# Three tiles of a row selection in f32r parts made on GpSimd, marks written on two engines, and a look-up one step earlier

## The reference

```python
gates = softmax(xf @ w_router + b_router)
topv, topi = top_k(gates, 2)                      # two experts per token
pos = cumsum(onehot)[...] - 1                     # running slot in each expert
keep = pos < cap                                  # cap = int(1.25 * 1184 / 8) = 185
buf = zeros(e, cap, d).at[e_flat, posc].add(where(keep, xf[tok], 0))
h = gelu(einsum('ecd,edf->ecf', buf, w1) + b1)    # 256 -> 1024
out = einsum('ecf,efd->ecd', h, w2) + b2          # 1024 -> 256
y = zeros.at[tok].add(w * out[e_flat, posc])      # weighted sum of the two experts
```

## Time and profile before

| | before |
|---|---|
| median of 3 runs, us | 159.71 (159.04 to 161.41) |
| span of the profiled execution, us | 157.9 |
| PE busy, us (share) | 148.0 (94%) |
| DVE busy | 105.5 (67%) |
| ACT busy | 82.8 (52%) |
| POOL busy | 50.9 (32%) |
| mean granted clock of PE | 0.989 |

### The profile page before, as it was taken

One profiled execution on the slowest core, in us unless ns is written; L12 is line 12 of the kernel. 1 busy time (PEld: TensorE's weight loads), 2 busy tenths in 40 slices (PEclk: granted clock), 3 DMA queues, 4 the chain that ended last, 5 costly groups with the idle time before them and its releaser, 6 DMA issues.

```text
span 157.9 us, 2961 instructions
## 1 busy us (share of the span) xinstructions
PE 148.0 (94%) x982; PEld 138.4 (88%) x982; DVE 105.5 (67%) x330; ACT 82.8 (52%) x210; POOL 50.9 (32%) x55
## 2 busy tenths in 40 slices
PE   7999999999999979999999999999999999999950
PEld 6548999899789768899799899999999999999940
DVE  0074994769887898981396859669486694785710
ACT  3222754644317998857066557474682665737100
POOL 6001200505530000005437167084371661604361
PEclk9999999999999999999999999999999999999995
DMA  5999960079000345301499897888868978600422
GB/s 169 406 420 435 394 230 0 0 243 338 5 0 22 138 163 184 116 0 28 97 349 292 272 269 194 269 192 307 269 130 270 262 250 264 131 7 0 48 25 23
DMA packets 16978, 28.46 MB, mean 180 GB/s; under 512 B 1133, under 2 KB 13591, under 8 KB 16585
## 3 DMA queue, kind: packets, MB, share of 16 engines
q1 hardware_dynamic: 14505, 25.49, 46.6%
q0 software_dynamic: 2464, 2.86, 10.6%
HBM read 24.21 MB, written 4.14 MB: 180 GB/s over the span
## 4 chain that ended last, share of the span: by engine, by line
PE 65%; DMA 11%; DVE 7%; ACT 6%; issue 3%; POOL 3%; SPq 1%; POOLq 1%; DVEq 0%
PE ps L1298 20%; PE ps L1333 10%; PE ps L1132 6%; PE ps L1223 6%; DMA w_even<-w 5%; DMA first_t<-first 4%; PE ps L1335 4%; PE ps L1240 3%; ACT xn L556 2%; PE ps L1165 2%; PE ps L1343 2%; PE ps L1310 2%; DMA rows_in<-xrows,src_row 2%; PE ps L1261 2%; ACT xn L565 2%
## 5 line engine op out<-in xcount | busy, mean ns | idle before, releaser
L497 POOL DMA_INDIRECT out_rows<-out_s,dst_row x16 | 23.8, 1485 | 38.4 <-ACT out_s L682 32.1
L658 ACT ACTIVATE first_t<-ps,b_cur 128x186 f32<-128x186 f32 x64 | 23.0, 413 | 23.5 <-PE ps L1298 22.0
L1333 PE MATMUL ps<-hid_hl,split 128*128 128x372 f32 x96 | 29.1, 369 | 0.0
L1335 PE MATMUL ps<-hid_hl,split 128*128 128x186 f32 x96 | 23.9, 249 | 0.0
L1298 PE MATMUL ps<-first_t,patch_t 128*128 128x186 f32 x128 | 21.7, 322 | 0.1
L977 DVE CAST hid_hl<-first_t 128x372 fp32r<-128x372 f32 x28 | 10.7, 383 | 15.9 <-ACT first_t L658 15.9
L1298 PEld LDWEIGHTS ps<-first_t,patch_t 128*128 128x128 f32 x128 | 20.1, 190 | 0.4 <-issue 0.4
L482 POOL DMA_INDIRECT rows_in<-xrows,src_row x14 | 15.6, 1113 | 11.0 <-DVE src_row L945 7.1
L1298 PE MATMUL ps<-first_t,w_even 128*128 128x186 f32 x112 | 18.9, 321 | 0.0
L522 ACT ACTIVATE split<-patch_t 128x512 fp32r<-128x512 f32 (+2 forms) x28 | 14.4, 577 | 8.1 <-DMA patch_t<-patches 5.7
L1335 PEld LDWEIGHTS ps<-hid_hl,split 128*128 128x128 f32 x96 | 18.3, 191 | 0.0
(11 more groups left out here) (179 smaller groups left out, 263.2 us busy)
## 6 DMA issues: line engine op xcount, KB each, us to landing
w_even<-w SPq DMA_DIRECT2D x8, 1024.0 KB, 5.7
patch_t<-w SPq DMA_DIRECT2D x8, 1024.0 KB, 5.5
att<-attn SPq DMA_DIRECT2D x1, 1280.0 KB, 9.4
patch_t<-patches SPq DMA_DIRECT2D x1, 1188.0 KB, 14.0
patch_t<-patches SPq DMA_DIRECT2D x1, 1080.0 KB, 11.5
first_t<-first SPq DMA_DIRECT2D x1, 978.0 KB, 7.0
out_rows<-h SPq DMA_DIRECT2D x2, 384.0 KB, 2.5
xrows<-xn SPq DMA_DIRECT2D x2, 384.0 KB, 3.5
```

The costliest lines, as they stand in the source:

```text
L497: pool.indirect_dma_start(out=out[:, :], out_offset=bass.IndirectOffsetOnAxis(ap=dst_row[0:SIZES[s], c:c + 1], axis=0), in_=out_s[q][0:SIZ ...
L658: ins = act.activation(hid[:, f, :], bank(pair)[:, (f % 2) * SL:(f % 2 + 1) * SL], ACT.Gelu, bias=b1_cur[q][:, f:f + 1])
L1333: pe.matmul(dst[:, 0:2 * SL], w2_h[q][:, f, cols], hid_hl[:, f].rearrange("p a s -> p (a s)"), start=f == 0, stop=False)
L1335: ins = pe.matmul(dst[:, 0:SL], w2_l[q][:, f, cols], hid_hl[:, f, 0], start=False, stop=f == KF - 1)
```

## The change

Tiles 6, 7 and 8 are selected in f32r: POOL copies each of them to a high part and subtracts that from the tile for a low part, as soon as ACT has written the tile; PE multiplies both parts by a one-hot matrix in f32r. The tiles of the second part come in the order 5, 9, 6, 7, 8, both halves of each together. In `ACT_ORDER`, `keep2` of E goes in front of `rows2` of C. POOL also writes `at_p` of tiles 7 and 8, the summand of L1028 and the first weight part; DVE writes `at_p` of the others and the last two weight parts, and its small operations on the weights move up by one place. ACT's load of the Gelu table goes behind its copy of half 1. The look-up goes in front of pair 3 of the first layer, and waits for POOL's writes too.

```diff
+PICK_PARTED = (6, 7, 8)
+PLACES = [*range(6), 9, *PICK_PARTED]
+BY_POOL = (7, 8)
...
+        pick_h, pick_l = (split[i][0:TT, 0:len(PICK_PARTED) * D].rearrange("p (t d) -> p t d", d=D) for i in (2, 3))
+        onehot_r = split[3][0:TT, len(PICK_PARTED) * D:len(PICK_PARTED) * (D + SL)].rearrange("p (t s) -> p t s", s=SL)
...
-                     ("rows2", B_), ("squares2", C), ("root2", C), ("rows2", C), ("keep2", E), ("rows2", E), ("keep2", C)]
+                     ("rows2", B_), ("squares2", C), ("root2", C), ("keep2", E), ("rows2", C), ("rows2", E), ("keep2", C)]
...
+            for i, t in enumerate(PICK_PARTED):
+                if t == GROUPS[C][0]:
+                    pool.wait_ge(row_made, 1)
+                elif t < GROUPS[E][0]:
+                    done(pool, ("rows2", C))
+                else:
+                    pool.wait_ge(row_made, 2)
+                pool.tensor_copy(pick_h[:, i], xn[:, t]).then_inc(row_high, 1)
+                pool.wait_ge(row_high, i + 1)
+                pool.tensor_tensor(pick_l[:, i], xn[:, t], pick_h[:, i], ALU.subtract).then_inc(row_split, 1)
+
+            pool.wait_ge(slots_fixed, 1)
+            for t in BY_POOL:
+                for k in range(2):
+                    pool.tensor_scalar(at_p[:, t, k], iota_slot[:, 0:ST], slot_p[:, t, k:k + 1], None, ALU.is_equal
+                                       ).then_inc(pool_marked, 1)
+            pool.wait_ge(places_known, 1)
+            for c in range(1, ID_SUM):
+                start = ids.rearrange("p (t c a b) -> p t c a b", c=ID_SUM, a=1, b=1)[:, :, c]
+                pool.tensor_tensor(marks[:, :, :, 1 + c], at_q, start.broadcast_to((TT, NT, 2, SC)), ALU.mult
+                                   ).then_inc(pool_marked, 1)
+            pool.wait_ge(first_part, 1)
+            pool.tensor_tensor(marks[:, :, :, ID_PARTS], at_q, spread(parts[:, :, :, 0], NT, SC), ALU.mult
+                               ).then_inc(pool_marked, 1)
...
-            act.activation(idle[:, :], eps_col[0:1], ACT.Gelu)
-
             act.wait_ge(picked, KD)
             copy(buf_t[0][:, 1:], pick_slot[:, 1:]).then_inc(half_ready, 1)
+
+            act.activation(idle[:, :], eps_col[0:1], ACT.Gelu)
...
-                for t in range(t0, t0 + n):
-                    dve.tensor_scalar(onehot[:, t], iota_slot[:, 1:SL + 1], place0[:, t:t + 1], None, ALU.is_equal
+                for t in PLACES[t0:t0 + n]:
+                    dst = onehot_r[:, PICK_PARTED.index(t)] if t in PICK_PARTED else onehot[:, t]
+                    dve.tensor_scalar(dst, iota_slot[:, 1:SL + 1], place0[:, t:t + 1], None, ALU.is_equal
...
             take_in(0, 0, first=True)
-            find_slots(0, 2)
+            find_slots(0, 1)
             behind(m)
             m = marked(dve.reciprocal(got[:, :], got[:, :]))
-            dve.wait_ge(places_known, 1)
-            for c in range(1, ID_SUM):
-                start = ids.rearrange("p (t c a b) -> p t c a b", c=ID_SUM, a=1, b=1)[:, :, c]
-                dve.tensor_tensor(marks[:, :, :, 1 + c], at_q, start.broadcast_to((TT, NT, 2, SC)), ALU.mult)
+            find_slots(1, 2)
+            behind(m)
+            m = marked(dve.tensor_tensor(weight[:, :, :], weight[:, :, :], per_token(got[:, :], 2), ALU.mult))
             find_slots(2, 3)
             behind(m)
-            m = marked(dve.tensor_tensor(weight[:, :, :], weight[:, :, :], per_token(got[:, :], 2), ALU.mult))
+            dve.tensor_copy(parts[:, :, :, 0], weight[:, :, :]).then_inc(first_part, 1)
             find_slots(3, 4)
...
-            find_slots(7, 9)
+            find_slots(6, BY_POOL[0])
             behind(m)
             m = part_of(2)
-            find_slots(9, NT)
+            find_slots(BY_POOL[-1] + 1, NT)
             behind(m)
-            for k in range(2):
-                ins = dve.tensor_tensor(marks[:, :, k, ID_PARTS:],
...
+            dve.wait_ge(places_known, 1)
+            for c in range(1, PARTS):
+                ins = dve.tensor_tensor(marks[:, :, :, ID_PARTS + c], at_q, spread(parts[:, :, :, c], NT, SC), ALU.mult)
             ins.then_inc(marks_ready, 1)
...
                 pe.wait_ge(pool_set, 10)
+                pe.wait_ge(pool_marked, 2 * len(BY_POOL) + ID_SUM)
...
-                pick_tiles(range(t0 - HELD, t0), range(KD))
-                for k in range(KD):
-                    pick_tiles(range(t0, t0 + c), [k]).then_inc(picked, 1)
+                pick_tiles([*range(t0 - HELD, t0), *(t for t in PLACES[t0:] if t not in PICK_PARTED)], range(KD))
+                for i, t in enumerate(PICK_PARTED):
+                    pe.wait_ge(onehot_ready, PLACES.index(t) + 1)
+                    pe.wait_ge(row_high, i + 1)
+                    for k in range(KD):
+                        pe.matmul(pick_slot[:, k, :], pick_h[:, i, k * 128:(k + 1) * 128], onehot_r[:, i, :],
+                                  start=False, stop=False)
+                    pe.wait_ge(row_split, i + 1)
+                    for k in range(KD):
+                        ins = pe.matmul(pick_slot[:, k, :], pick_l[:, i, k * 128:(k + 1) * 128], onehot_r[:, i, :],
+                                        start=False, stop=t == PICK_PARTED[-1])
+                        if t == PICK_PARTED[-1]:
+                            ins.then_inc(picked, 1)
...
                     up(e, q, pair, not first)
+                if first:
+                    look_up(bank(MARKS_BANK)[0:ST, 0:(ID_PARTS + PARTS) * SC])
                 up(e, q, PAIRS - 1, not first)
                 if first:
-                    look_up(bank(MARKS_BANK)[0:ST, 0:(ID_PARTS + PARTS) * SC])
```

More of the change, by code:

```diff
@@ L264, in vit_block @@
         onehot_ready, picked = sem("onehot_ready"), sem("picked")
+        row_made, row_high, row_split = sem("row_made"), sem("row_high"), sem("row_split")
         places_known, rows_marked = sem("places_known"), sem("rows_marked")
+        slots_fixed, first_part, pool_marked = sem("slots_fixed"), sem("first_part"), sem("pool_marked")
         marks_ready, marks_looked, src_ready, dst_ready = (
@@ L566, in normalise @@
                                          bias=nmr[0:r, base + t:base + t + 1], scale=rstd[0:r, base + t:base + t + 1])
+                    if base and t in PICK_PARTED and i < n - 1:
+                        ins.then_inc(row_made, 1)
                 return ins
@@ L1012, in _ @@
             behind(n)
-            n = marked(dve.tensor_tensor(slot_p[:, :, :], slot_p[:, :, :], lost[:, :, :], ALU.add))
+            dve.tensor_tensor(slot_p[:, :, :], slot_p[:, :, :], lost[:, :, :], ALU.add).then_inc(slots_fixed, 1)
             behind(m)
             m = marked(dve.tensor_tensor(got[:, :], weight[:, :, 0], weight[:, :, 1], ALU.add))
-            behind(n)
+            dve.wait_ge(slots_fixed, 1)
             dve.tensor_tensor(at_q[:, :, :, :], grid(iota_slot[:, 0:SC], NT, 2, SC), spread(slot_q[:, :, :], NT, SC), ALU.is_equal
@@ L1021, in _ @@
             take_in(0, 0, first=True)
-            find_slots(0, 2)
+            find_slots(0, 1)
             behind(m)
             m = marked(dve.reciprocal(got[:, :], got[:, :]))
-            dve.wait_ge(places_known, 1)
-            for c in range(1, ID_SUM):
-                start = ids.rearrange("p (t c a b) -> p t c a b", c=ID_SUM, a=1, b=1)[:, :, c]
-                dve.tensor_tensor(marks[:, :, :, 1 + c], at_q, start.broadcast_to((TT, NT, 2, SC)), ALU.mult)
+            find_slots(1, 2)
+            behind(m)
+            m = marked(dve.tensor_tensor(weight[:, :, :], weight[:, :, :], per_token(got[:, :], 2), ALU.mult))
             find_slots(2, 3)
             behind(m)
-            m = marked(dve.tensor_tensor(weight[:, :, :], weight[:, :, :], per_token(got[:, :], 2), ALU.mult))
+            dve.tensor_copy(parts[:, :, :, 0], weight[:, :, :]).then_inc(first_part, 1)
             find_slots(3, 4)
-            behind(m)
-            m = part_of(0)
+            dve.wait_ge(first_part, 1)
+            m = rest_after(0)
             find_slots(4, 5)
             behind(m)
-            m = rest_after(0)
+            m = part_of(1)
             find_slots(5, 6)
             behind(m)
-            m = part_of(1)
-            find_slots(6, 7)
-            behind(m)
             m = rest_after(1)
-            find_slots(7, 9)
+            find_slots(6, BY_POOL[0])
             behind(m)
             m = part_of(2)
-            find_slots(9, NT)
+            find_slots(BY_POOL[-1] + 1, NT)
             behind(m)
-            for k in range(2):
-                ins = dve.tensor_tensor(marks[:, :, k, ID_PARTS:],
-                                        at_q[:, :, k].rearrange("p t (a q) -> p t a q", a=1).broadcast_to((TT, NT, PARTS, SC)),
-                                        parts[:, :, k].rearrange("p t (c a) -> p t c a", a=1).broadcast_to((TT, NT, PARTS, SC)),
-                                        ALU.mult)
+            dve.wait_ge(places_known, 1)
+            for c in range(1, PARTS):
```

(17 more changed lines are left out.)

## The result

The changed kernel took 163.11 us (median of 4 runs, 160.94 to 164.35), the kernel before 159.38 beside it (4 runs). The ratio is 1.0146 [1.0096, 1.0197]: slower, by less than 2%. Two of the four executions (163.84, 164.35) had a granted clock of 0.97 in the mean, as some executions of the kernel before have too; the ratio leaves these out, the median doesn't. The profiled execution took 160.94, with a span of 159.1 against 157.9. On the page POOL's busy time rises from 50.9 to 58.2 us and PE's falls from 148.0 to 147.4.

A forecast was written before the change was run, and what follows sets the result against it. Bound by DVE's string up to the take-in, then by whether marks are ready for PE. Terms 1.5 + 0.3 + 1.6 - 0.3 = +3.1 us, span near 161.0, time 162.8; forecast's own range 161.6 to 164.2, overall range 159.6 to 164.9.

The forecast's parts named there:

- held in front, free behind: Rival: the parts cost 1.15 before the take-in, POOL's marks run freely behind it, look-up waits 0.3; 161.2 us, chance 0.20.
- A two-operand DVE operation stands until POOL's has ended.: Between 60 and 70 us, DVE operations with two SBUF operands stand still until the POOL operation in progress ends.
- The parts, +1.5.: Ahead of the take-in, POOL's three copies and three subtracts hold DVE's string: +1.5 us (1.15 to 1.85).
- Pick on PE, 0.: The f32r pick on PE, even if shorter, gains 0, since the take-in was not waiting for it.
- POOL's is_equal in front of the take-in, +0.3.: POOL's first is_equal holds the next small DVE operation in front of the take-in: +0.3 us (0 to 0.7).
- The wait at the look-up, 1.6: Marks come 5.8 after the take-in, PE is at the look-up 4.16 after it: PE waits 1.6 (0 to 3.0).
- 2.56 held: Behind the take-in, POOL's three is_equal (0.8) and two products (1.76) hold DVE for 2.56, about 0.3 of it harmless.
- What POOL's marks give.: DVE's marks work gets 1.33 shorter by durations, about 1.1 with overlap, but POOL's operations among it hold DVE.
- The look-up earlier, -0.3.: Ahead of pair 3: no wait for gathered rows, expert 2's weights load earlier, expert 1's output wait goes; -0.3 (-0.6 to 0).
- The clock, rival at 0.18.: Rival: PE idle before the first layer lowers its clock, up to +2.4; 164.5 us, 165.2 at the outside, chance 0.18.

The follow-up runs named there:

- e1: The change without POOL's copies and subtracts, tiles picked in f32 as before; POOL's marks and the earlier look-up stay: 159.64 us, ratio 1.0027.
- e10: e1 with POOL's three copies and three subtracts put back, their results read by nobody: 160.77 us, ratio 1.0104.
- e2: The change with DVE writing the marks that POOL writes there; POOL's copies and subtracts and the earlier look-up stay: 161.80 us, ratio 1.0105.
- e8: e5 with two more filler products on PE ahead of the first part of the pick: 159.57 us, ratio 1.0001.
- e9: The change with two more filler products on PE ahead of the first part of the pick: 161.55 us, ratio 1.0081.
- e6: The kernel before, with the look-up in front of pair 3 and nothing else: 160.58 us, ratio 1.0006.
- e5: The change without POOL's copies and subtracts, POOL keeping only the four is_equal of at_p; DVE writes the marks products: 159.57 us, ratio 0.998.
- e7: The kernel before, with four unread is_equal of 128x96 added on POOL near 32 us, nothing beside them: one run, 161.09 us.
- change_again: The change once more, unaltered, run beside e10 and e11 against the kernel before: 161.78 us, ratio 1.0155.
- e11: e1 with six unread is_equal of 96 elements on POOL at the moments of the copies and subtracts: 159.74 us, ratio 1.0003.

## Why the prediction came out as it did, step by step

The direction, the place and, in front of the take-in, the mechanism were right; the sum was twice too large. The traces give +1.56 where the sum was +3.1. That the median of 163.11 lies near the 162.8 is luck: two of its four executions had the lower mean clock, which is no part of the sum. In size the trace is at the rival "held in front, free behind" (161.2), although DVE was held behind too.

- *A two-operand DVE operation stands until POOL's has ended.* Right for POOL's two-operand operations and its copies, by the five ends above; a copy cost chosen only 0.08 because it was nearly done. Too wide as a rule: POOL's is_equal held hardly anything, its memsets nothing of this kind.
- *The parts, +1.5.* Right, and somewhat less: +1.19 (+1.26 against e1). The terms are is_one +0.36, chosen +0.08, `below` +0.55, and 0.47 on the one-hots, taken at 0.35 in the middle of its bounds; against it stand some 0.2 for which DVE had waited ahead of `place`. The copy was 0.40 as estimated. (The sum's lower bound doesn't follow from its own times: one-hots at 63.63 instead of 62.40 are 1.23 late, not 1.15.)
- *Pick on PE, 0.* Right: e10.
- *POOL's is_equal in front of the take-in, +0.3.* Wrong: 0. It started at 65.94, beside at_q, which took its 0.49, while the is_equal took 0.84.
- *The wait at the look-up, 1.6: the term most off.* PE came to it 4.17 after the take-in's end, as forecast (4.16). The marks were ready 4.80 after it, not 5.8. The step that failed was "2.56 held": the four is_equal took 2.62, not 4 x 0.27, for which the prediction itself would have a wait near 3.0, but they held nothing; only the two products (1.57) held, 0.54 on an at_p and 0.53 on `weight`. DVE's own work was 3.73 (forecast 3.5). The row shows 0.69 of idle; first layer and look-up together are 0.96 longer, the other 0.27 mostly because the products on both sides of the stop no longer overlap.
- *What POOL's marks give.* 4.65 from the take-in's end to the marks before, 4.80 after: what POOL takes over and what it holds cancel, as e2 says too.
- *The look-up earlier, -0.3.* The size was too small (-0.60), and both reasons failed. The wait for the rows stayed at 0.4, since they landed 5.8 after the look-up's end instead of 4.6, with the load of instructions over their gather; in e8 and e9, where it is over before, the wait goes, as forecast. Expert 2's weights were issued no earlier against PE (1.28 after the rows' transposes begin, before and after: the second of two loads, issued at 78.03 and 79.78). The 0.48 behind that came because the load landed in 7.1 instead of 7.6, and the wait at expert 1's output vanished; e6, whose load took 7.7, kept it. Why the loads differ isn't shown.
- *The clock, rival at 0.18.* Not seen at its place: PE stood 1.32, not 2.2, and a window of the changed kernel (length, then busy PE, PEld, DVE, ACT, POOL, granted clock, DMA) shows the full clock behind it:

```profile
67.00:68.00 1.00, 1.00 (x7) 1.00 (x8) 1.00 (x6) 0.85 (x3) 1.00 (x2) 1.00 0.00 0
```

Open: why POOL's is_equal, which reads SBUF, doesn't hold DVE; the Trainium skill's rule in the section named above would have it hold at_p, and the measured 0.34 to 0.42 decides against it here. Open too: why the load of instructions comes when it does. No version tried beats the kernel before beyond its interval; e5 is the nearest.

## What to carry to other kernels

An engine that idles beside a critical string of DVE is not free: before giving work to GpSimd, go through DVE's operations in that stretch, their number of SBUF operands and GpSimd's kind of operation, and add up what is held. Take the hold from rows of that same pair of operations; a two-operand subtract says nothing of an is_equal or a memset. What is held is what is left of GpSimd's operation when DVE's begins. A step moved forward gains only if what it starts also lands earlier, so look at the landing, not at the issue, and at what else the DMA queues carry then.

## What was not expected of the hardware

- GpSimd's is_equal of 128x96 takes 0.51 us alone and 0.65 in the change; a copy of 256 elements takes 0.40 and a two-operand subtract of 256 takes 0.73. Its price doesn't follow from the elements.
- A load of the program's own instructions can hold up a gather. In nine of the thirteen traces it lies over expert 1's gather, and the rows land 5.3 to 5.8 after the look-up's end; in the other four (before, e7, e8, e9) it is over by the gather's first packet, and they land 4.5 to 4.7 after it. No run moves the load alone, so this is shown by the order of events only.
- PE's clock falls, in some executions only, in a gap that the kernel before has too, ahead of the first part of the pick. In the profile of change_again PE was busy for 0.62 of the us from 57 to 58 and stood 0.85 ahead of 58.78; the granted clock went to 0.50, the lower level (1.2 GHz), and that part of the pick took 4.83 instead of 3.42. Windows of change_again, columns as above:

```profile
57.00:58.00 1.00, 0.62 (x10) 0.37 (x9) 0.93 (x8) 1.00 (x5) 0.00 (x0) 1.00 0.77 263
...
59.00:59.50 0.50, 0.50 (x2) 0.50 (x3) 0.50 (x3) 0.50 (x4) 0.00 (x0) 0.50 0.00 0
```

In the change's first profile the same gap, 0.86, and the later one of 1.32 passed at 1.00. The fall cost the change little: take-in 7.67 behind the reciprocal instead of 7.35, last out_s 91.78 instead of 91.69. In e11's profile, where that part of the pick took 6.31, the last out_s came 92.80 behind it, 2.5 later than in e1.
